# First pair pass of a four-layer graph network: one slab's subtraction on GpSimd, own values from PSUM, slabs in the order 0, 2, 1, 3

## What is computed

```
D = jnp.abs(x[:, :, None, :] - x[:, None, :, :])          # all pairs of nodes of a graph
h = jnp.einsum('bijc,oc->bijo', D, W1) + b1               # 128 channels to 64
m = jnp.mean(h, axis=(0, 1, 2)); v = jnp.mean((h - m) ** 2, axis=(0, 1, 2))
h = leaky((h - m) / jnp.sqrt(v + EPS) * g1 + be1)         # then scores, softmax, two products
```

## The kernel before

|x_i - x_j| is symmetric, so for each graph only 64 cyclic distances are made, in `SLABS` = 4 slabs. A slab is 128 channels x 2048 columns: two halves of eight distances x 128 nodes. `hd` holds each graph's channels x nodes with the first 64 nodes repeated behind them, so that a slab is one instruction over two views of it, the node's own values and a shifted window (`windows`).

## Time and profile before

### The profile page before, as it was taken

One profiled execution on the slowest core, in us unless ns is written; L12 is line 12 of the kernel. 1 busy time (PEld: TensorE's weight loads), 2 busy tenths in 40 slices (PEclk: granted clock), 3 DMA queues, 4 the chain that ended last, 5 costly groups with the idle time before them and its releaser, 6 DMA issues. The chain is left out here.

```text
span 2237.3 us, 43782 instructions
## 1 busy us (share of the span) xinstructions
PE 1857.5 (83%) x13411; PEld 1155.8 (52%) x13419; DVE 1892.8 (85%) x2726; ACT 1568.4 (70%) x3389; POOL 334.0 (15%) x282
## 2 busy tenths in 40 slices
PE   2978888888867888886799999999999577877886
PEld 2857777777754555665544444444444233333346
DVE  5978888888876999997899999999999466666766
ACT  0634554455436888883499999999999577777773
POOL 1510000000001110103322222222221000000001
PEclk9979999999986999996699999999999799999998
DMA  6000000000000000000155555555555799999982
GB/s 170 0 8 1 1 0 0 0 0 0 0 1 13 6 4 5 5 5 19 49 209 204 216 202 211 206 212 204 212 206 206 268 358 349 345 353 348 353 288 78
DMA packets 122539, 297.25 MB, mean 133 GB/s; under 512 B 20352, under 2 KB 56456, under 8 KB 122264
## 3 DMA queue, kind: packets, MB, share of 16 engines
q1 hardware_dynamic: 105336, 287.69, 34.3%
q10 hardware_dynamic: 16896, 8.39, 1.3%
q0 software_dynamic: 256, 0.56, 0.1%
HBM read 154.78 MB, written 141.82 MB: 133 GB/s over the span
## 5 line engine op out<-in xcount | busy, mean ns | idle before, releaser
L1239 DVE TENSOR_TENSOR v_pairs<-hd 128x2048 f32 (+1 forms) x128 | 291.8, 2280 | 0.0
L1244 DVE TENSOR_TENSOR v_pairs<-hd 128x2048 f32 (+1 forms) x128 | 291.4, 2277 | 0.0
L1300 ACT ACTIVATE v_hid<-v_psW 128x1024 f32<-128x1024 f32 x256 | 265.5, 1037 | 18.1 <-PE v_psW L1341 9.6
L724 DVE TENSOR_REDUCE m_part<-m_psS 128x128 f32<-128x1024 f32 (+1 forms) x192 | 216.9, 1130 | 67.1 <-PE m_psS L603 67.0
L1341 PE MATMUL v_psW<-v_pairs,p_w1T 128*64 128x512 f32 x1024 | 247.5, 600 | 26.8 <-DVE v_pairs L1239 26.8
L1303 ACT ACTIVATE v_junk<-v_psW 128x1024 bf16<-128x1024 f32 x256 | 266.4, 1041 | 0.0
L603 PE MATMUL m_psS<-m_onehot,m_tableT 64*128 64x128 f32 x2816 | 217.3, 293 | 34.2 <-DVE m_part L724 18.0
L1341 PE MATMUL v_psW<-v_pairs,l_w1T 128*64 128x512 f32 (+1 forms) x1024 | 243.2, 587 | 0.0
L956 ACT ACTIVATE a_ex<-a_eu,a_nmx 128x128 f32<-128x128 f32 x512 | 197.8, 390 | 42.2 <-PE a_psA L925 34.3
L1224 POOL COPY v_weights<-p_split 128x192 bf16 (+1 forms) x64 | 154.0, 2407 | 476.9 <-PE v_psW L1341 466.6
L1483 DVE SCALAR_TENSOR_TENSOR s_hid<-s_hid 128x1024 f32<-128x1024 f32 x128 | 155.8, 1221 | 66.6 <-ACT s_hid L1543 66.6
(11 more groups left out here) (251 smaller groups left out, 3573.9 us busy)
## 6 DMA issues: line engine op xcount, KB each, us to landing
pair_hidden<-v_hid SPq DMA_DIRECT2D x256, 512.0 KB, 2.6
s_h<-pair_hidden SPq DMA_DIRECT2D x128, 1024.0 KB, 7.4
s_wide<-pair_scores SPq DMA_DIRECT2D x64, 128.0 KB, 6.0
adj_ring<-in_adj_dram ACTq DMA_DIRECT2D x16, 256.0 KB, 5.0
x_all<-in_x_dram ACTq DMA_DIRECT2D x16, 256.0 KB, 5.3
out_dram<-o_res SPq DMA_DIRECT2D x16, 256.0 KB, 2.3
pair_scores<-s_rot SPq DMA_DIRECT2D x64, 32.0 KB, 6.0
p_ends<-in_c_ends_dram SPq DMA_DIRECT2D x1, 1024.0 KB, 4.7
```

What stands on the lines that cost most here:

```text
L724: nc.vector.tensor_reduce(part[:, i, r, :], psS[:, 2 * (at % 2):2 * (at % 2) + 2, 0:w].rearrange("z q (c i) -> z i q c", i=N), AX.XY, ALU. ...
L1239: nc.vector.tensor_tensor(slab(s), one, far, ALU.max).then_inc(max_done, 1)
L1244: nc.vector.tensor_tensor(slab(s), one, far, ALU.subtract).then_inc(sub_done, 1)
L1300: nc.scalar.activation(hid[:, s, :], psW[:, buf, :], ACT.Identity, accum_out=hsum[:, bass.ds(m, 1)]).then_inc(evacuated, 1)
```

## The change

Per graph:

- GpSimd subtracts slab 3, which gets two homes in `D` (slots 3 and 4 in turn). It waits until VectorE has done both ANDs of the graph before, and until the product two graphs back has been taken from that home.
- VectorE copies a graph's own values (128 columns) into PSUM (`psX`, two halves in turn) a graph ahead, and uses them as first input of its two maxima and its subtraction. It now does both ANDs, of slab 1 and of slab 3. Its order is maximum 0, maximum 2, subtract 1, copy, AND 1, AND 3.
- TensorE, ScalarE and SP take the slabs in the order 0, 2, 1, 3; ScalarE's absolute value is gone.
- `hd` is N columns longer (the copy ahead of the last graph reads them; VectorE clears them), four graphs stand in front of the loop and its body holds six.

```diff
+        D = sb("pairs", [C, SLABS + 1, SC])
+        psX = k.ps(ctx, "v_psX", [C, 2, N])
+        ORDER = (0, 2, 1, 3)
+        home = lambda u, s: s + u % 2 if s == SLABS - 1 else s
         def graphs(eng, step):
-            step(0, 0)
-            with eng.Fori(0, (B - 1) // 3) as t:
-                for u in range(3):
-                    step(3 * t + (u + 1), (u + 1) % 3)
+            for n in range(4):
+                step(n, n)
+            with eng.Fori(0, (B - 4) // 6) as t:
+                for u in range(4, 10):
+                    step(6 * t + u, u)
...
+                def step(n, u):                                   # GpSimd
+                    pool.wait_ge(w_mm, done(n * SLABS - (2 * SLABS + 3)))
+                    nc.gpsimd.tensor_copy(weights[:, u % 3, :], split[:, bass.ds(n * (3 * HID), 3 * HID)]).then_inc(weighed, 1)
+                    one, far = windows(hd, n, SLABS - 1)
+                    pool.wait_ge(vabs_done, done(2 * n - 1))
+                    pool.wait_ge(w_mm, done((n - 2) * SLABS + 3))
+                    nc.gpsimd.tensor_tensor(D[:, home(u, SLABS - 1), :].rearrange("c (h d i) -> c h d i", h=2, i=N), one, far,
+                                            ALU.subtract).then_inc(psub_done, 1)
...
+                def ahead(n, u):                                  # VectorE
+                    nc.vector.tensor_copy(psX[:, u % 2, :], hd[:, bass.ds(n * DUP, N)]).then_inc(one_ready, 1)
+                def step(n, u):
+                    own = psX[:, u % 2, :].unsqueeze(1).unsqueeze(1).broadcast_to([C, 2, DS, N])
                     def larger(s):
-                        one, far = windows(hd, n, s)
-                        dve.wait_ge(w_mm, done((n - 1) * SLABS + s))
-                        nc.vector.tensor_tensor(slab(s), one, far, ALU.max).then_inc(max_done, 1)
...
-                    subtract(VABS)
+                        dve.wait_ge(w_mm, done((n - 1) * SLABS + s // 2))
+                        nc.vector.tensor_tensor(slab(s), own, windows(hd, n, s)[1], ALU.max).then_inc(max_done, 1)
+                    def absolute(slot):
+                        bits = D[:, slot, :].bitcast(I32)
+                        nc.vector.tensor_scalar(bits, bits, 0x7FFFFFFF, None, ALU.bitwise_and).then_inc(vabs_done, 1)
+                    dve.wait_ge(one_ready, done(n))
                     larger(0)
-                    dve.wait_ge(sub_done, done(2 * n))
-                    bits = D[:, VABS, :].bitcast(I32)
-                    nc.vector.tensor_scalar(bits, bits, 0x7FFFFFFF, None, ALU.bitwise_and).then_inc(vabs_done, 1)
-                    subtract(AABS)
                     larger(2)
+                    dve.wait_ge(w_mm, done((n - 1) * SLABS + 2))
+                    nc.vector.tensor_tensor(slab(1), own, windows(hd, n, 1)[1], ALU.subtract).then_inc(sub_done, 1)
+                    ahead(n + 1, u + 1)
+                    dve.wait_ge(sub_done, done(n))
+                    absolute(1)
+                    dve.wait_ge(psub_done, done(n))
+                    absolute(home(u, 3))
...
-                        if s == 0:                                # ScalarE
-                            act.wait_ge(sub_done, done(2 * n + 1))
-                            nc.scalar.activation(D[:, AABS, :], D[:, AABS, :], ACT.Abs).then_inc(aabs_done, 1)
...
-                            pe.wait_ge(vabs_done if s == VABS else aabs_done, done(n))
+                            pe.wait_ge(vabs_done, done(2 * n + s // 2))
```

More of the change, by code:

```diff
@@ L1052, in phase_pairs @@
     with ExitStack() as ctx:
-        hd = k.sb(ctx, "hd", [C, B * DUP], F32)
+        hd = k.sb(ctx, "hd", [C, B * DUP + N], F32)
         alpha = k.sb(ctx, "p_alpha", [N, 1], F32)
@@ L1175, in phase_pair_hidden @@
         sb = lambda name, shape, dt=F32: k.sb(ctx, "v_" + name, shape, dt)
-        D = sb("pairs", [C, SLABS, SC])
+        D = sb("pairs", [C, SLABS + 1, SC])
         hid = sb("hid", [N, SLABS, HALF])
@@ L1189, in phase_pair_hidden @@
         psS = k.ps(ctx, "v_psS", [N, 512])
+        psX = k.ps(ctx, "v_psX", [C, 2, N])
         sem = lambda name: k.sem("v_" + name)
-        cleared, consts, sub_done, vabs_done, aabs_done, max_done, w_mm, evacuated, squared, totals, folded, algebra, rooted, own_mm = (sem(n) for n in (
-            "cleared", "consts", "sub_done", "vabs_done", "aabs_done", "max_done", "w_mm", "evacuated", "squared", "totals", "folded", "algebra", "rooted", "own_mm"))
+        cleared, consts, sub_done, psub_done, vabs_done, max_done, one_ready, w_mm, evacuated, squared, totals, folded, algebra, rooted, own_mm = (sem(n) for n in (
+            "cleared", "consts", "sub_done", "psub_done", "vabs_done", "max_done", "one_ready", "w_mm", "evacuated", "squared", "totals", "folded", "algebra", "rooted", "own_mm"))
         weighed = sem("weighed")
@@ L1195, in phase_pair_hidden @@
         PAIRS = float(B * N * N)
-        VABS, AABS = 1, 3
+        ORDER = (0, 2, 1, 3)
+        home = lambda u, s: s + u % 2 if s == SLABS - 1 else s
         def graphs(eng, step):
-            step(0, 0)
-            with eng.Fori(0, (B - 1) // 3) as t:
-                for u in range(3):
-                    step(3 * t + (u + 1), (u + 1) % 3)
+            for n in range(4):
[3 more added lines that the diff above has]
+                    step(6 * t + u, u)
         with nc.Block() as block:
@@ L1212, in _ @@
                 for m in range(B * SLABS):
+                    s = ORDER[m % SLABS]
                     sp.wait_ge(evacuated, done(m))
-                    sp.dma_start(hidden[m], hid[:, m % SLABS, :]).then_inc(stored[m % SLABS], 16)
+                    sp.dma_start(hidden[m // SLABS * SLABS + s], hid[:, s, :]).then_inc(stored[s], 16)
                 for s in range(SLABS):
@@ L1219, in _ @@
             def _(pool):
[L1220 to L1224, removed]
+                for s in (weighed, psub_done):
+                    pool.sem_inc(s, BIAS)
+                def step(n, u):
[6 more added lines that the diff above has]
+                                            ALU.subtract).then_inc(psub_done, 1)
                 graphs(pool, step)
@@ L1228, in _ @@
             def _(dve):
-                for s in (sub_done, vabs_done, max_done):
+                for s in (sub_done, vabs_done, max_done, one_ready):
                     dve.sem_inc(s, BIAS)
                 nc.vector.memset(none[:, :], 0.0)
+                nc.vector.memset(hd[:, B * DUP:B * DUP + N], 0.0)
                 nc.vector.memset(ones[:, :], 1.0).then_inc(cleared, 1)
                 slab = lambda s: D[:, s, :].rearrange("c (h d i) -> c h d i", h=2, i=N)
-                def step(n, buf0):
+                def ahead(n, u):
+                    nc.vector.tensor_copy(psX[:, u % 2, :], hd[:, bass.ds(n * DUP, N)]).then_inc(one_ready, 1)
@@ L1252, in _ @@
+                    absolute(1)
+                    dve.wait_ge(psub_done, done(n))
+                    absolute(home(u, 3))
+                ahead(0, 0)
                 graphs(dve, step)
@@ L1290, in _, with step @@
             def _(act):
-                for s in (aabs_done, evacuated, squared):
+                for s in (evacuated, squared):
                     act.sem_inc(s, BIAS)
[L1294 to L1297, removed]
+                def step(n, u):
+                    for at, s in enumerate(ORDER):
+                        m = n * SLABS + at
+                        buf = (u + at) % 3
                         act.wait_ge(w_mm, done(m))
@@ L1302, in step @@
                         act.wait_ge(squared, done(m - 2))
-                        nc.scalar.activation(junk[:, s % 2, :], psW[:, buf, :], ACT.Square,
+                        nc.scalar.activation(junk[:, at % 2, :], psW[:, buf, :], ACT.Square,
                                              accum_out=hsq[:, bass.ds(m, 1)]).then_inc(squared, 1)
-                        if s == 0:
-                            act.wait_ge(sub_done, done(2 * n + 1))
-                            nc.scalar.activation(D[:, AABS, :], D[:, AABS, :], ACT.Abs).then_inc(aabs_done, 1)
                 graphs(act, step)
@@ L1316, in _, with step @@
                 pe.wait_ge(cleared, 1)
-                def step(n, buf0):
+                def step(n, u):
                     pe.wait_ge(weighed, done(n))
-                    for s in range(SLABS):
-                        m = n * SLABS + s
-                        buf = (buf0 + s) % 3
+                    for at, s in enumerate(ORDER):
+                        m = n * SLABS + at
+                        buf = (u + at) % 3
                         width = lambda c, half: TAIL - 512 if s == SLABS - 1 and half and c else 512
@@ L1331, in step @@
                                         col = (s + half) * HALF + c
-                                        nc.tensor.matmul(psW[half * HID:half * HID + HID, buf, c:c + 512], weights[:, buf0, t * HID:(t + 1) * HID], ends[:, col:col + 512],
```

(3 more changed lines are left out.)

## The result

Four runs of the changed kernel have a median of 2193.78 us (2191.81 to 2195.47), four of the kernel before 2234.99 (2232.70 to 2235.16): 41.2 us less, ratio 0.9814, 95% interval 0.9801 to 0.9828. The forecast was 2191.7 in a range of 2187 to 2216; the result lies 2.1 us above it, inside the range. The profiled execution took 2195.21 us, its span is 2193.4.

The account below looks back on a forecast made before the run. VectorE bounds the pass at 10.09 us a graph, TensorE afterwards at 9.42. Gains of 41.9 (steady part), 1.0 (first graph) and 0.3 us (ScalarE's end), together 43.2, take 2234.93 to 2191.7 us; range 2187 to 2216.

Parts of the forecast that it names:

- The profiled execution: The single traced run of the whole kernel: span forecast to go from 2237.3 to 2194.1 us, own time to 2195.9.
- VectorE was the bound, TensorE is: First pair pass: VectorE sets 10.09 us a graph before the change, TensorE 9.42 after; chance 0.73.
- VectorE's 9.08 us: VectorE's need per graph after the change: 6.60 two-input instructions, 2.28 ANDs, 0.20 copy into PSUM.
- TensorE's 9.42 us: TensorE's need per graph: two end-node lots at 1.29, three products at 1.72, slab 3's at 1.68 us.
- GpSimd's 4.16 us: GpSimd's subtraction of slab 3, estimated as 4 x 1.04 us a graph, hidden beside VectorE's PSUM-fed work.
- No exclusion with the PSUM input: GpSimd's subtraction runs beside VectorE's two maxima and subtraction (6.6 us), since their first input is in PSUM; cost nothing.
- the slow rival: GpSimd and VectorE exclude each other despite the PSUM input: 13.24 us a graph, 2433 us; chance 0.05.
- ScalarE's absolute value had to go too: Dropping the 1.91 us absolute value takes ScalarE from 9.95 to 8.04 us a graph.
- First graph 11.4 us: TensorE's first graph of the pass falls from 12.40 to 11.4 us, as a maximum comes first; gain 1.0.
- ScalarE's tail: End of the pass: ScalarE, no longer behind with its queue, ends some 0.3 us nearer to the last product.
- The back edge: Rival: the loop's back edge stalls TensorE, nine times at 2 us, 18 us in all, giving 2210; chance 0.05.
- VectorE's lead: VectorE runs ahead until slab 2's home is not free, idles 0.34 us a graph; slab 3 ready some 4 us early.

Follow-up runs that it names:

- the run with two parts: Changed kernel with two of the three bf16 parts in the end-node matmuls, 8 instead of 12 for slabs 0 and 2; 2166.28 us, ratio 0.9691.

## Why the prediction was right, step by step

- **VectorE was the bound, TensorE is.** Right: TensorE is full at 200.00 us and without waits, and the run with two parts, where less work for TensorE makes the kernel faster, shows it from the other side.
- **VectorE's 9.08 us.** It is 9.06 in the first six graphs, where VectorE isn't held, and in the run with two parts. The PSUM input costs nothing (2.28 us), the ANDs start 1.14 us apart, and the copy into PSUM is 0.28 us long.
- **TensorE's 9.42 us** is the mis-sized term: it is 9.46. I had taken 1.68 us for slab 3 off the starts in the earlier trace rows, but there the starts told of the shorter half, and the other one has the full width. 63 x 0.04 = 2.5 us; the steady part took 595.98 us against 593.61 worked out. The median came out 2.1 us above the forecast.
- **The profiled execution** hides this miss by luck: its span of 2193.4 us lies under the 2194.1 worked out only because its pass began 2.5 us earlier.
- **GpSimd's 4.16 us.** It is 4.21 on average, and hidden. The 4497 ns of the Trainium skill (GPSIMD Engine Reference, 3.1) is 7% above this. Its section 4.1 prefers VectorE for such work because GpSimd takes about twice as long; the trace agrees, 4.21 us beside 2.28, and the time was still free here because GpSimd had stood idle 3/4 of the window of the earlier trace rows.
- **No exclusion with the PSUM input**, the point on which the slow rival hung: shown by the run that takes that input away.
- **ScalarE's absolute value had to go too.** Right in kind; it added 1.80 us to ScalarE's graph, not 1.91, which matters only in the run that gives it back.
- **First graph 11.4 us**, measured 11.56, with two terms off in opposite directions: the first lot took 1098.20 - 1095.64 = 2.56 us for 2.77, the slow product 1100.80 - 1098.20 = 2.60 for 2.2.
- **ScalarE's tail:** VectorE's first reduction starts 1706.06 - 1703.18 = 2.88 us after the last matmul, 0.4 less than before, for 0.3 forecast.
- **The back edge.** No stall shows: the first eight turns behind the first graph take 9.40 to 9.41 us and all later ones 9.45 to 9.46, whatever their place in a body of six.
- **VectorE's lead.** It is idle 0.31 us a graph, for 0.34 forecast. By 9.46 less 9.06 it should be 0.40: the starts of the two maxima lie 1406.75 - 1404.16 = 2.59 us apart in place of 2.20, so the trace counts the wait 0.08 us shorter than the delay. Slab 3 is ready 3.5 us before its product (1404.24 to 1407.79), for some 4 forecast.

## What to carry to other kernels

Where two engines keep each other out, look at which operands do it: VectorE's two-input instructions let GpSimd run beside them once one input comes from PSUM, and a copy of 128 columns was enough for three instructions of 2048. Moving work off the bound is worth only the distance to the next engine, so write down every engine's need per turn first, and relieve the second one in the same edit. With single buffers give producer and consumer the same order, and sum the ring of waits with its handovers. For two matmul streams take the longer stream's need, from its widths and not from start times. No run here takes away the second home of slab 3 or the longer loop body, so what these two are worth is not shown.

## What the runs showed that I had not expected

Matmuls for output partitions 0 to 63 and 64 to 127 slip against each other over graphs when one half has less to do, from 0 to some 0.4 us, and starts then show the shorter half's period of 9.41 us for eight turns before the true one of 9.46. GpSimd's instruction that is started 3.0 us into VectorE's stretch of PSUM-fed work (1410.72 after 1407.76), without any wait for the ANDs, lengthened the two ANDs by 0.40 us only and the kernel not at all.
